# A conditional residual kernel: the LoRA factor that carries the condition, the last four LoRA products by pairs, and the place of the bias sums

## The reference

```python
def _L0_cond_ref(x, y, weight, mask, bias):
    masked_w = weight * mask[None, :, :]
    w_bot = jnp.einsum('bg,got->bot', y, masked_w)
    return jnp.einsum('bnt,bot->bno', x, w_bot) + bias

def _L1_cond_ref(x, w, W_base, b_base, As, Bs):
    SCALING = 2.0
    out = jnp.einsum('btc,oc->bto', x, W_base) + b_base
    h = jnp.einsum('btc,erc->bter', x, As)
    lora = jnp.einsum('bter,eor,be->bto', h, Bs, w)
    return out + lora * SCALING

x = x + _L0_cond_ref(x, cond_8, L0_cond_weight, L0_cond_mask, L0_cond_bias)
x = x + _L1_cond_ref(x, cond_8, L1_cond_W_base, L1_cond_b_base, L1_cond_As, L1_cond_Bs)
```

## Time and profile before

| | us |
|---|---|
| median of 3 runs | 57.27 (57.02 to 57.6) |
| the profiled execution | 57.23 |
| its span | 55.4 |

### The profile page before, as it was taken

How to read it: one execution, slowest core, us unless ns; L and a number is a source line. 1 busy time by engine, 2 the same in 40 slices (tenths; PEclk the granted TensorE clock), 3 DMA queues, 4 the chain that set the end, 5 groups by cost and what they waited for, 6 DMA issues and landing times.

```text
span 55.4 us, 997 instructions
## 1 busy us (share of the span) xinstructions
PE 51.7 (93%) x342; PEld 47.1 (85%) x342; DVE 42.1 (76%) x64; ACT 31.5 (57%) x52; POOL 31.2 (56%) x30
## 2 busy tenths in 40 slices
PE   2999999999999999999999999999999999999900
PEld 2988999999999888988998898899889889888800
DVE  0039999979596998999999999979929959805030
ACT  1949900447807889440999925970993950840800
POOL 4003400299980099999909999999966990000000
PEclk9999999999999999999999999999999999999999
DMA  0699999999999994000082540090054045049572
GB/s 0 133 392 335 373 366 389 419 418 425 408 396 417 417 393 169 9 0 0 0 306 78 222 169 0 15 364 0 6 195 183 0 185 194 0 179 382 197 284 95
DMA packets 5476, 11.79 MB, mean 213 GB/s; under 512 B 608, under 2 KB 1376, under 8 KB 5472
## 3 DMA queue, kind: packets, MB, share of 16 engines
q1 hardware_dynamic: 5184, 11.35, 54.6%
q10 hardware_dynamic: 288, 0.39, 1.9%
HBM read 7.54 MB, written 4.19 MB: 212 GB/s over the span
## 4 chain that ended last, share of the span: by engine, by line
PE 93%; DVE 1%; issue 0%
PE ps_out L441 13%; PE ps_out L483 13%; PE ps_out L445 13%; PE ps_out L449 13%; PE ps_merge L441 7%; PE ps_merge L445 7%; PE ps_merge L449 7%; PE ps_merge L522 6%; PE ps_lora L441 5%; PE ps_lora L445 5%; PE ps_lora L449 5%; DVE out_sb L432 1%; PE ps_lora L547 1%; DVE warm L310 0%
## 5 line engine op out<-in xcount | busy, mean ns | idle before, releaser
L189 POOL TENSOR_TENSOR W_lo<-W,W_hi 128x512 fp32r<-128x512 f32 x8 | 10.5, 1314 | 7.1 <-ACT W_hi L235 7.1
L342 DVE TENSOR_TENSOR x_lo<-x_sb,x_hi 128x1024 fp32r<-128x1024 f32 x8 | 12.7, 1584 | 0.0
L195 POOL TENSOR_TENSOR W_lo<-W,W_hi 128x512 fp32r<-128x512 f32 x6 | 10.9, 1824 | 0.0
L441 PE MATMUL ps_out<-x_hi,M_hi 128*128 128x512 f32 (+1 forms) x32 | 9.8, 388 | 0.0
L445 PE MATMUL ps_out<-x_lo,M_hi 128*128 128x512 f32 (+1 forms) x32 | 9.7, 384 | 0.0
L449 PE MATMUL ps_out<-x_hi,M_lo 128*128 128x512 f32 (+1 forms) x32 | 9.7, 384 | 0.0
L248 ACT ACTIVATE M_hi<-ps_merge 128x512 fp32r<-128x512 f32 x8 | 4.8, 597 | 8.0 <-PE ps_merge L449 8.0
L255 ACT ACTIVATE x_hi<-x_sb 128x1024 fp32r<-128x1024 f32 x8 | 8.4, 1053 | 0.0
L199 POOL TENSOR_TENSOR W<-W,ident 128x256 f32<-128x256 f32 x6 | 6.6, 1099 | 3.0 <-DVE x_lo L342 3.0
L357 DVE TENSOR_SCALAR out_sb<-ps_out,bias_sb 128x512 f32<-128x512 f32 x7 | 5.2, 747 | 3.5 <-PE ps_out L449 3.4
L264 ACT ACTIVATE out_sb<-ps_out,bias_sb 128x512 f32<-128x512 f32 x8 | 5.5, 685 | 3.9 <-PE ps_out L449 2.2
(11 more groups left out here) (50 smaller groups left out, 80.1 us busy)
## 6 DMA issues: line engine op xcount, KB each, us to landing
x_sb<-xT_dram SPq DMA_DIRECT2D x8, 512.0 KB, 10.2
outT_dram<-out_sb SPq DMA_DIRECT2D x15, 256.0 KB, 2.3
packs_sb<-packs_dram SPq DMA_DIRECT2D x7, 288.0 KB, 5.3
rows_sb<-rows_dram SPq DMA_DIRECT2D x1, 384.0 KB, 6.8
base_sb<-base_dram ACTq DMA_DIRECT2D x1, 256.0 KB, 3.6
outT_dram<-out_sb SPq DMA_DIRECT2D x2, 128.0 KB, 1.8
packs_sb<-head_dram SPq DMA_DIRECT2D x1, 192.0 KB, 3.4
packs_sb<-rest_dram SPq DMA_DIRECT2D x1, 160.0 KB, 3.6
```

The costliest lines, as they stand in the source:

```text
L189: pool.tensor_tensor(W1_lo[:, b % W1BUF], W1[:, b % W1BUF], W1_hi[:, b % W1BUF].bitcast(f32), ALU.subtract).then_inc(w1lo_done, 1)
L195: pool.tensor_tensor(W0_lo[:, b % 2], W0[:, b], W0_hi[:, b % 2].bitcast(f32), ALU.subtract).then_inc(w0lo_done, 1)
L342: nc.vector.tensor_tensor(x_lo[:, b % XBUF], x_sb[:, b], x_hi[:, b % XBUF].bitcast(f32), ALU.subtract).then_inc(xlo_done, 1)
L441: nc.tensor.matmul(out, hi_l, hi_r, start=(n == 0), stop=False)
```

## The change

1. The condition scales B instead of A. A gets the factor 2 once, on VectorE (`A_hi`, `A_lo`, one each); `B_hi(b)` is made for each batch by ScalarE, `B_lo(b)` by VectorE. ScalarE waits for both factor loads before the first.
2. The LoRA products of batches 4 to 7 go by pairs: as A is now the stationary factor of all batches, and B of neighbouring batches lies side by side, one matmul has 512 columns. `lora_pair(4)` stands in lora(4)'s place, `lora_pair(6)` behind apply(2). Half j of both batches goes into `ps_lora[j]`.
3. `w1_pair(b)` evacuates a pair in two instructions, one for each j, each for both batches; it stands behind m_lo in VectorE's rounds 1 and 3. ScalarE's w1_hi of batches 4 and 5 waits for both, and so for 6 and 7.
4. The bias sums lie in `ps_out[3]`. TensorE waits for `bias_done` before the second half of apply(1), which writes that bank; lora(5)'s wait is gone. The two base dots now come after the bias matmuls.
5. ScalarE copies bias0's row into the same bank of PSUM, ahead of the W0_hi halves of the ramp, and the three dots read it there.

```diff
--- before.py
+++ after.py
@@ -29,7 +29,7 @@
     EXPW = KQ * C
     PACKW = EXPW + NT * TQ
     SCALING = 32.0 / 16
-    LEAD = 4
+    SINGLE = 4
     XBUF = 4
     W1BUF = 4
     WARM = 28
@@ -79,10 +79,10 @@
         base_bias0 = sb("base_bias0", [P, NT])
         low_bias = sb("low_bias", [P, NB])
         bias_sb = sb("bias_sb", [P, NT, NB])
-        B_hi = sb("B_hi", [P, C], f32r)
-        B_lo = sb("B_lo", [P, C], f32r)
-        A_hi = sb("A_hi", [P, NB, C], f32r)
-        A_lo = sb("A_lo", [P, NB, C], f32r)
+        A_hi = sb("A_hi", [P, C], f32r)
+        A_lo = sb("A_lo", [P, C], f32r)
+        B_hi = sb("B_hi", [P, NB, C], f32r)
+        B_lo = sb("B_lo", [P, NB, C], f32r)
         W1 = sb("W1", [P, W1BUF, NT, C])
         W1_hi = sb("W1_hi", [P, W1BUF, NT, C], f32r)
         W1_lo = sb("W1_lo", [P, W1BUF, NT, C], f32r)
@@ -107,7 +107,9 @@
         ps_mix = ps_out
         ps_last = ps_lora[0][:, 0, :]
 
-        ps_bias = ps_lora[1][:, 0, 0:NT * NB].rearrange("p (j b) -> p j b", j=NT)
+
+        ps_bias = ps_out[3][:, 0:NT * NB].rearrange("p (j b) -> p j b", j=NT)
+        ps_row = ps_out[3][:, C:2 * C]
 
 
 
@@ -119,7 +121,7 @@
 
         warm_set, ident_zero, ident_done = sem("warm_set"), sem("ident_zero"), sem("ident_done")
         base_done, dots_done, low_done, fixed_done = sem("base_done"), sem("dots_done"), sem("low_done"), sem("fixed_done")
-        bias_mm, bias_done, bhi_done, blo_done = sem("bias_mm"), sem("bias_done"), sem("bhi_done"), sem("blo_done")
+        row_done, bias_mm, bias_done, bhi_done, blo_done = sem("row_done"), sem("bias_mm"), sem("bias_done"), sem("bhi_done"), sem("blo_done")
 
         ahi_done, alo_done = sem("ahi_done"), sem("alo_done")
         lora_mm, w1_done, w1hi_done, w1lo_done = sem("lora_mm"), sem("w1_done"), sem("w1hi_done"), sem("w1lo_done")
@@ -223,12 +225,12 @@
 
         @block.scalar
         def _(act):
-            def a_hi(b):
-                nc.scalar.activation(A_hi[:, b], A_er, ACT.Copy,
-                                     scale=cond_er[:, b:b + 1]).then_inc(ahi_done, 1)
+            def b_hi(b):
+                nc.scalar.activation(B_hi[:, b], B_er, ACT.Copy,
+                                     scale=cond_er[:, b:b + 1]).then_inc(bhi_done, 1)
 
             def w1_hi(b):
-                act.wait_ge(w1_done, b + 1)
+                act.wait_ge(w1_done, b + 1 if b < SINGLE else b // 2 * 2 + 2)
 
                 if b >= W1BUF:
                     act.wait_ge(merge_mm, b - W1BUF + 1)
@@ -270,9 +272,10 @@
             nc.scalar.activation(table_sb[:, :], warm[:, 0:1], ACT.Copy)
             act.dma_start(base_sb[:, :, :], base.rearrange("p (j o) -> p j o", j=NT)).then_inc(base_in, 16)
 
+            act.wait_ge(B_arrived, 16)
             act.wait_ge(lora_arrived, 16)
             for b in range(NB):
-                a_hi(b)
+                b_hi(b)
             w1_hi(0)
             w1_hi(1)
 
@@ -280,6 +283,10 @@
             nc.scalar.activation(W0_hi[:, 0:2, :, 0:H], W0[:, 0:2, :, 0:H], ACT.Copy).then_inc(ramp_hi, 1)
             w1_hi(2)
             split_x_hi(0)
+
+            act.wait_ge(rows_in, 16)
+            act.wait_ge(w0_done, NQ)
+            nc.scalar.activation(ps_row, bias0_row, ACT.Copy).then_inc(row_done, 1)
             for b in range(2):
                 act.wait_ge(eye_second, 1)
                 nc.scalar.activation(W0_hi[:, b, :, H:C], W0[:, b, :, H:C], ACT.Copy).then_inc(ramp_hi, 1)
@@ -309,19 +316,25 @@
         def _(dve):
             nc.vector.memset(warm[:, :], 0.0).then_inc(warm_set, 1)
 
-            def a_lo(b):
-                dve.wait_ge(ahi_done, b + 1)
-                nc.vector.scalar_tensor_tensor(out=A_lo[:, b], in0=A_er, scalar=cond_er[:, b:b + 1],
-                                               in1=A_hi[:, b].bitcast(f32),
-                                               op0=ALU.mult, op1=ALU.subtract).then_inc(alo_done, 1)
+            def b_lo(b):
+                dve.wait_ge(bhi_done, b + 1)
+                nc.vector.scalar_tensor_tensor(out=B_lo[:, b], in0=B_er, scalar=cond_er[:, b:b + 1],
+                                               in1=B_hi[:, b].bitcast(f32),
+                                               op0=ALU.mult, op1=ALU.subtract).then_inc(blo_done, 1)
 
             def w1(b):
                 dve.wait_ge(lora_mm, b + 1)
-                if b >= W1BUF:
-
-                    dve.wait_ge(w1lo_done, b - W1BUF + 1)
-                nc.vector.tensor_tensor(W1[:, b % W1BUF], ps_lora[b % 2][:, :, :], base_sb[:, :, :],
+                nc.vector.tensor_tensor(W1[:, b], ps_lora[b % 2][:, :, :], base_sb[:, :, :],
                                         ALU.add).then_inc(w1_done, 1)
+
+            def w1_pair(b):
+                dve.wait_ge(lora_mm, SINGLE + (b - SINGLE) // 2 + 1)
+                dve.wait_ge(w1lo_done, b - W1BUF + 2)
+                at = b % W1BUF
+                for j in range(NT):
+                    nc.vector.tensor_tensor(W1[:, at:at + 2, j, :], ps_lora[j][:, :, :],
+                                            base_sb[:, j, :].unsqueeze(1).to_broadcast([P, 2, C]),
+                                            ALU.add).then_inc(w1_done, 1)
 
             def w0(q):
                 dve.wait_ge(mix_mm, q + 1)
@@ -359,7 +372,7 @@
 
             def dot(row, out):
 
-                return nc.vector.tensor_tensor_reduce(out=row_products[:, :], in0=row, in1=bias0_row, scale=1.0,
+                return nc.vector.tensor_tensor_reduce(out=row_products[:, :], in0=row, in1=ps_row, scale=1.0,
                                                       scalar=0.0, op0=ALU.mult, op1=ALU.add, accum_out=out)
 
             def ramp_low(b):
@@ -367,14 +380,14 @@
                 nc.vector.tensor_tensor(W0_lo[:, b, :, H:C], W0[:, b, :, H:C], W0_hi[:, b, :, H:C].bitcast(f32),
                                         ALU.subtract).then_inc(ramp_lo, 1)
 
+            dve.wait_ge(lora_arrived, 16)
+            nc.vector.tensor_scalar(A_hi[:, :], A_er, SCALING, None, ALU.mult).then_inc(ahi_done, 1)
+            dve.wait_ge(ahi_done, 1)
+            nc.vector.scalar_tensor_tensor(out=A_lo[:, :], in0=A_er, scalar=SCALING, in1=A_hi[:, :].bitcast(f32),
+                                           op0=ALU.mult, op1=ALU.subtract).then_inc(alo_done, 1)
             dve.wait_ge(B_arrived, 16)
-            nc.vector.tensor_scalar(B_hi[:, :], B_er, SCALING, None, ALU.mult).then_inc(bhi_done, 1)
-            dve.wait_ge(bhi_done, 1)
-            nc.vector.scalar_tensor_tensor(out=B_lo[:, :], in0=B_er, scalar=SCALING, in1=B_hi[:, :].bitcast(f32),
-                                           op0=ALU.mult, op1=ALU.subtract).then_inc(blo_done, 1)
-            dve.wait_ge(lora_arrived, 16)
             for b in range(NB):
-                a_lo(b)
+                b_lo(b)
             nc.vector.tensor_tensor(bias_sum[:, :], bias0, bias1, ALU.add).then_inc(fixed_done, 1)
             dve.wait_ge(fixed_done, 1)
             w0(0)
@@ -398,6 +411,7 @@
             split_x_lo(0)
             m_lo(0)
 
+            dve.wait_ge(row_done, 1)
             dve.wait_ge(rows_in, 16)
             dot(A_er, A_bias0[:, :]).then_inc(dots_done, 1)
             dve.wait_ge(dots_done, 1)
@@ -407,12 +421,11 @@
             m_lo(1)
             split_x_lo(1)
 
+            dve.wait_ge(bias_mm, 1)
             for j in range(NT):
                 dve.wait_ge(dots_done, 1 + j)
                 dot(base_rows[:, j, :], base_bias0[:, j:j + 1]).then_inc(dots_done, 1)
             dve.wait_ge(dots_done, 1 + NT)
-
-            dve.wait_ge(bias_mm, 1)
             for j in range(NT):
                 last = nc.vector.tensor_scalar(bias_sb[:, j, :], ps_bias[:, j, :], base_bias0[:, j:j + 1],
                                                bias_sum[:, j:j + 1], ALU.add, ALU.add)
@@ -420,11 +433,11 @@
             dve.wait_ge(bias_done, 1)
             for b in range(1, NB):
                 out1(b - 1)
-                if b + 3 < NB:
-                    w1(b + 3)
                 if b + 1 < NB:
                     split_x_lo(b + 1)
                     m_lo(b + 1)
+                if b == 1 or b == 3:
+                    w1_pair(b + 3)
 
             b = NB - 1
             dve.wait_ge(apply_mm, 2 * b + 3)
@@ -451,19 +464,27 @@
 
             def lora(b):
 
-                pe.wait_ge(ahi_done, b + 1)
+                pe.wait_ge(bhi_done, b + 1)
                 if b == 0:
-                    pe.wait_ge(bhi_done, 1)
+                    pe.wait_ge(ahi_done, 1)
                 if b >= 2:
                     pe.wait_ge(w1_done, b - 1)
-                if b == 5:
-                    pe.wait_ge(bias_done, 1)
                 for j in range(NT):
                     cols = slice(j * P, (j + 1) * P)
                     mm = product(ps_lora[b % 2][:, j, :],
-                                 [(A_hi[:, b, cols], A_lo[:, b, cols], B_hi[:, :], B_lo[:, :])],
-                                 lo_ready=(alo_done, b + 1),
```

(23 more changed lines are left out.)

## The result

| | before | after |
|---|---|---|
| median us | 57.20 (13 runs) | 57.57 (13 runs) |
| profiled execution, us | 57.23 | 57.94 |
| its span, us | 55.4 | 56.2 |

The ratio is 1.0067, 95% interval 1.0035 to 1.0098: 0.38 us slower (0.20 to 0.56), within the 1% of "no change" and, seen over 13 runs, on the slower side. 57.7 us was predicted. Now and then an execution takes over 1 us more, with either kernel; the ratios leave these out.

The account below looks back on a forecast made before the run. TensorE's queue from first matmul to last, plus one evacuation, was taken to bound the kernel. -0.14 - 0.10 + 0.04 + 0.64 = +0.44 us on the 57.27 median gave 57.7 us, own range 57.4 to 58.0, with rivals 56.95 to 58.3.

Parts of the forecast that it names:

- two pairs for four singles: On TensorE, 24 products of 256 columns become 12 of 512: 0.14 us gained, bounds 0 and 0.14.
- small stall at the second merge halves: On TensorE in the ramp, the wait for W0_hi goes as the merge moves 0.65 later: -0.10 us, bounds 0 and -0.10.
- bias_done before apply(1)'s second half: TensorE's new wait: bias_done at 25.45, the half due at 25.87, so no cost.
- wait in merge(4): TensorE needs W0_lo(4) at 33.27 and waits until 33.85, plus 0.06 for a weight load: +0.64 us.
- start: First product 0.18 later, as ScalarE waits for both factor loads; +0.04 us, bounds -0.05 and +0.30.
- The deciding term: W1 for batches 4 to 7: late evacuation delays W0_lo(4) on GpSimd to 33.75 or 33.85, TensorE waits: +0.64 us.
- The blocking of GpSimd and VectorE: When both read two SBUF tensors, the first holds the other off; the blocked one ends its length less 0.14 later.
- rival (b): Bias wait ahead of apply(1)'s second half bites if dots stay stretched: 0.7 in the middle, 58.35 us; chance 0.08.
- The gap between matmuls: On TensorE, rows show about 0.012 us for each matmul fewer; the skill's 2.5 ns would give 0.03 us for 12.
- PSUM as a source: VectorE's three dots lose their second SBUF operand: 0.70 us taken per dot with read-out; rows disagree with the skill's penalty.
- a first lora slower by over 0.1: At TensorE's start, a sign that would show the prediction wrong: a first lora slower by more than 0.1.
- No second stall: W0_lo(5) ready at 38.05, merge(5), already 0.64 late, asks at 38.1: no further wait on TensorE.

Follow-up runs that it names:

- e1: Changed kernel with w1_pair moved right behind out1 in VectorE's rounds 1 and 3, ahead of x_lo and M_lo: 56.83 us, ratio 0.9896 to the kernel before.
- e9: Kernel before, without any part of the change, with w1(b+3) moved behind M_lo in VectorE's rounds: 59.90 us, ratio 1.0374.
- e2: Changed kernel with only GpSimd's order altered, W0_lo(4) ahead of W1_lo(4): 56.86 us, ratio 0.9900 to the kernel before.
- e5: Changed kernel without the copy of bias0's row into PSUM, the three dots reading it in SBUF: 59.60 us, ratio 1.0387 to the kernel before.
- e3: Kernel before with part 1 of the change alone, the condition scaling B: 57.51 us, ratio 1.0030.
- e6: Changed kernel with x_lo(3) moved on VectorE from round 2 to round 3, behind out1(2): 57.70 us, ratio 1.0104 to the kernel before.

## Why the prediction was right

Point by point, from the profiled executions (times of after beside the earlier trace rows):

| step | predicted us | measured us |
|---|---|---|
| two pairs for four singles | -0.14 | 1.39 + 1.36 - 2.88 = -0.13 |
| small stall at the second merge halves | -0.10 | (20.00 - 18.40) - (19.18 - 17.46) = -0.12 |
| bias_done before apply(1)'s second half | 0 | 0 |
| wait in merge(4) | +0.64 | 2.13 - 1.44 = +0.69 |
| start | +0.04 (-0.05 to +0.30) | 15.49 - 15.23 = +0.26 |
| sum | +0.44 | +0.70; by the ratio +0.38 |

- **The deciding term** came as forecast: halves of W1 ending at 29.82 (29.6 forecast, at a start 0.04 late; the profile's start was 0.26 late), W0_lo(4) at 34.02 (33.75), W1_lo(4) stretched to 2.21. e1 and e9 show that the place of the evacuation makes it, with the pairs and without them; e2 shows that it goes through GpSimd's order.
- **The blocking of GpSimd and VectorE**, read from two pairs of rows, was the right rule: less the later start, stretched operations ended within 0.1 us of where it put them. e5 shows it from the other side. The dots were mis-sized both ways: 0.70 with the read-out had been taken for one with the row in PSUM, and the next starts 0.45 behind it (0.41 for the dot itself); and rival (b), had it come, would have cost 1.7 by e5, not 0.7. The first error changed nothing, by luck: x_lo(2) could begin earlier, but GpSimd held it until 26.94 all the same.
- **The gap between matmuls**: two pairs save 0.13, so the rows' price, about 0.01 us for each matmul saved, holds. By the fixed cost that the Trainium skill states in TensorE: Matmul & The Clock Gate, on the gap between matmuls, it would have been 0.03 in all; here the measurement decides.
- **PSUM as a source**: a dot with its row in PSUM takes 0.41 us against 0.66 to 1.50 from SBUF in the kernel before and in e5, each time beside a busy GpSimd. (The Trainium skill, VectorE: DVE Perf Modes, on the TRN2 errata, would have it some 0.065 us slower than from SBUF; no run here has an unblocked dot from SBUF to compare.)
- **The start** was the loosest term. In the profile it cost 0.26, near the upper bound. The prediction named a first lora slower by over 0.1 as a sign of being wrong, and in the profile lora(1) does start 0.13 later (6.03 against 5.90); the other 0.13 comes from a pace that doubles later (a step of 0.12 to 0.13 us from 6.65 on, in the kernel before from 6.27). Over all executions it can't have cost 0.26: 0.38 less the queue's +0.46 leaves about -0.1 (interval -0.26 to +0.10), and e3's spans give 0.04. So between 0 and 0.1 fits both, as forecast, but a single execution says little about it, and that the median came within 0.13 us of the forecast is in part the luck of this term.
- **"No second stall"** was right for the changed kernel (W0_lo(5) at 38.21, asked for at 38.35), for the reason given, that the first one had been paid: e6 removes the first and gets the second, of 0.65.

## What to carry to other kernels

Where one engine's queue holds operations for two consumers, an operation that becomes ready later delays everything behind it there: ask of a postponed evacuation not whether its own reader can wait, but what stands behind it in each queue that it feeds. A saving on the bounding engine of 0.01 us a matmul is real, but one VectorE instruction in the wrong place costs it several times over; move the place first, then count matmuls. And when a hole is closed, add up the queue that made it over the next round too: if its work doesn't fit, the hole comes back one round later, as in e6.
